# Sixteen strip copies of a fill, issued so that neighbours use different partition halves

## The reference, cut to what matters

```
x = x + L0_conv(group_norm(x))
t = to_tokens(x)                        # [16, 3136, 32]
t = t + attention(layer_norm(t))        # 32 features, softmax over 3136 keys
t = t + experts(layer_norm(t))          # top 2 of 8
x = from_tokens(t)

def L0_conv(x):                         # n c h w
    t1 = stack of x shifted by 2k-6 columns, k = 0..6
    t2 = conv(x, w2, 1x3)
    t3 = einsum('nakhw,nbhw->nakb', t1, x) / sqrt(h*w)
    t4 = stack of t2 shifted by k-3 rows, k = 0..6
    t7 = conv(t2, w7, 1x5, one filter per channel)
    t8 = conv(x, w8, 5x5, dilation 2, one filter per channel)
    t10 = einsum('nakb,nakhw->nbhw', p9w*p6w*t3, t4) / sqrt(c*7)
    return t8 - (t10 - t7)
```

## Time and profile before

| | |
|---|---|
| median of 3 runs | 2959.19 us |
| the profiled execution's own time | 2957.68 us |
| its span | 2955.7 us |
| busy: PE, DVE, ACT, POOL | 84%, 81%, 56%, 9% |
| first stage | 0 to about 655 us |
| copies of SyncE and ScalarE | 220.95 MB, mean 75 GB/s |

### The profile page before, as it was taken

The page is one execution under the profiler, slowest core; times in us unless marked ns, Lnnn a source line. Parts: engine busy times, 40 slices in busy tenths (PEclk is TensorE's granted clock), DMA queues, the critical chain, the costliest instruction groups (busy, mean ns, idle before and its releaser), DMA issues. The chain is left out here.

```text
span 2955.7 us, 47695 instructions
## 1 busy us (share of the span) xinstructions
PE 2474.4 (84%) x18582; PEld 990.8 (34%) x18582; DVE 2393.8 (81%) x4202; ACT 1649.4 (56%) x2170; POOL 276.4 (9%) x273
## 2 busy tenths in 40 slices
PE   3858585734599999999999999999999997787776
PEld 1332323210122222222222222222222226666664
DVE  4466666558899999999999999999999804888787
ACT  1243424350177777777777777777777793333322
POOL 0000000010000000000000000000000002454455
PEclk9989788855599999999999999999999995666667
DMA  7885859142001103110110110111010002221210
GB/s 167 186 218 163 221 157 240 72 157 74 1 1 56 56 1 116 56 37 20 56 56 1 56 56 15 42 56 56 1 56 23 4 20 77 69 96 66 99 66 22
DMA packets 61174, 220.95 MB, mean 75 GB/s; under 512 B 15526, under 2 KB 28450, under 8 KB 54306
## 3 DMA queue, kind: packets, MB, share of 16 engines
q1 hardware_dynamic: 59762, 214.41, 24.7%
q10 hardware_dynamic: 1200, 3.69, 0.3%
HBM read 81.67 MB, written 74.60 MB: 53 GB/s over the span
## 5 line engine op out<-in xcount | busy, mean ns | idle before, releaser
L1121 DVE TENSOR_REDUCE at_XM<-at_psX 128x1 f32<-128x448 f32 x2688 | 1551.9, 619 | 69.6 <-PE at_psX L1001 41.6
L1071 ACT ACTIVATE at_PR<-at_psS 128x896 f32<-128x896 f32 x1344 | 1159.3, 915 | 370.9 <-PE at_psS L980 368.6
L1017 PE MATMUL at_psV<-at_PR,at_V 128*32 128x448 f32 x5376 | 645.2, 552 | 0.5 <-ACT at_PR L1071 0.5
L980 PE MATMUL at_psS<-at_US,at_KS 128*128 128x448 f16 x2688 | 630.8, 356 | 2.5 <-ACT at_PR L1071 0.9
L1001 PE MATMUL at_psX<-at_KS,at_US 64*128 64x448 f16 x1344 | 501.9, 373 | 83.4 <-DVE at_XM L1121 76.7
L1001 PE MATMUL at_psX<-at_KS,at_UH 64*128 64x448 f16 x1344 | 501.8, 373 | 0.0
L1001 PEld LDWEIGHTS at_psX<-at_KS,at_US 64*128 64x128 f16 x1344 | 125.2, 93 | 751.9 <-DVE at_XM L1121 719.6
L980 PEld LDWEIGHTS at_psS<-at_US,at_KS 128*128 128x128 f16 x2688 | 205.1, 98 | 288.5 <-ACT at_PR L1071 140.4
L1396 POOL TENSOR_TENSOR fi_WE<-fi_WE 128x256 f32<-128x256 f32 (+1 forms) x224 | 212.8, 978 | 172.6 <-DVE fi_WE L1450 171.9
L393 PE MATMUL psA<-sb_stacks,sb_lhs 128*32 128x448 f32 x1568 | 170.2, 563 | 15.5 <-DVE sb_X L766 8.0
L1450 DVE TENSOR_TENSOR fi_WE<-fi_psE,fi_WT 128x512 f32<-128x512 f32 (+1 forms) x208 | 132.5, 665 | 43.4 <-PE fi_psE L1299 34.3
(11 more groups left out here) (186 smaller groups left out, 2000.5 us busy)
## 6 DMA issues: line engine op xcount, KB each, us to landing
sums<-at_O SPq DMA_DIRECT2D x16, 1568.0 KB, 6.3
fi_SUMS<-sums SPq DMA_DIRECT2D x16, 1568.0 KB, 6.6
sb_stacks<-sb_T SPq DMA_DIRECT2D x64, 270.5 KB, 5.8
sb_stacks<-sb_Xp SPq DMA_DIRECT2D x64, 248.8 KB, 5.0
sb_stacks<-sb_Xp SPq DMA_DIRECT2D x64, 248.0 KB, 4.9
at_KS<-key_stacks SPq DMA_DIRECT2D x16, 784.0 KB, 7.8
at_US<-query_stacks SPq DMA_DIRECT2D x16, 784.0 KB, 10.1
sb_stacks<-sb_T SPq DMA_DIRECT2D x64, 172.5 KB, 3.8
```

Of the source, the lines that this page charges most:

```text
L980: last = nc.tensor.matmul(psS[:, i % 2, j, 0:TILE], KS[:, b, c * P:(c + 1) * P], US[:, b, t * TILE:(t + 1) * TILE], start=True, stop=True)
L1017: last = nc.tensor.matmul(psV[C * q:C * q + C, 0:TILE], V[:, b, G * k + q, :], PR[:, (2 * q4 + q // 2) % PRS, q % 2, :], start=(k == 0), s ...
L1071: nc.scalar.activation(PR[:, (i - 2) % PRS], psS[:, i % 2, :, 0:TILE], ACT.Exp).then_inc(p_ready, 1)
L1121: nc.vector.tensor_reduce(o, psX[:, (at + j) % 3, 0:TILE], AX.X, ALU.max).then_inc(x_done, 1)
```

## The change

The two fills loop over one list of pairs instead of two nested loops. The same 16 copies are issued, with the same sizes, semaphores and waits before them; only their order within a fill differs.

```
+        HG = G // 2
+        STRIP_ORDER = [p for k in range(G) for j in range(HG) for p in ((j, (HG + j + k) % G), (HG + j, (j + k) % G))]
...
             def fill_stacks(g, h):
                 a, z = (0, XS_CUT) if h == 0 else (XS_CUT, XS_LEN)
-                for n in range(G):
-                    for s in range(G):
-                        sp.dma_start(XS[C * s:C * s + C, n, a:z],
-                                     Xp[C * n:C * n + C, 2 * s + a:2 * s + z]).then_inc(xs_in[h], 16)
+                for n, s in STRIP_ORDER:
+                    sp.dma_start(XS[C * s:C * s + C, n, a:z],
+                                 Xp[C * n:C * n + C, 2 * s + a:2 * s + z]).then_inc(xs_in[h], 16)
```

More of the change, by code:

```diff
@@ L274, in fill_stacks2 @@
                 sp.wait_ge(t2_ready, g * NT + (3 if h == 0 else NT))
[L275 to L278, removed]
+                for n, s in STRIP_ORDER:
+                    sp.dma_start(T2S[C * s:C * s + C, n, a:z],
+                                 T2[C * n:C * n + C, YW * s + a:YW * s + z]).then_inc(t2s_in[h], 16)
             def store(m, n, z=first, alone=False):
```

## The result

The changed kernel takes **2933.88 us** (median of 4 runs, 2933.05 to 2934.96), against 2958.86 us (2957.76 to 2959.78) for the kernel before in the same session: ratio 0.9918, 95% interval 0.9906 to 0.9931. That is 25 us less, where 49 were forecast, and 12 us above the top of the forecast's own range (2896 to 2922). The profiled execution took 2934.68 us with a span of 2932.7, 23.0 us less than before.

The account below looks back on a forecast made before the run. Bound by strip copies at 206 GB/s, on which TensorE and, through SyncE's queue, VectorE's token loads wait. Savings of 7.9 + 14.9 + 14.4 + 12.0 = 49.2 us over four passes gave 2910 us, range 2896 to 2922.

Parts of the forecast that it names:

- What bounds the kernel: Strip copies on SyncE's queue, at 206 GB/s, hold up TensorE's x strips and VectorE's token loads.
- That the sequencer is held back by the copies: SyncE's strip issue: median 1212 ns against shortest 582 ns, read as waiting for the copies ahead.
- The price of a strip: Time per x-stack strip: from 1.23 us to 0.80 us, taken between 0.70 and 0.92.
- The lone microsecond at 270 GB/s: First pass, 35 to 36 us, at the seam of strips 8 and 9: worth 0.31 us per seam.
- rival (a): Strip fills: a seam helps little, strips at 1.16 to 1.2 us, about 2949 us; chance 0.16.
- The passes: Savings forecast for the first four passes: 7.9, 14.9, 14.4 and 12.0 us, sum 49.2 us.
- The token wait of the third pass: VectorE's 11.7 us wait for the token load was to go, with 2.5 us to spare.
- the 1.6 us forecast there: Third pass, ScalarE's first eviction: held by a query store until 290.73, T2's clearing ends at 289.06.
- rival (b): Strip fills: half the gain, strips at 1.0 to 1.05 us, 30 us saved, 2929 us; chance 0.17.
- the five signs: 32 strips issued in about 26 us, rate near 300 GB/s, convolution at 38 to 39 us, short token waits, sb_T release.
- Over 1.1 us a strip: Strip fills: the forecast is wrong if a strip still takes over 1.1 us.
- The slower rival: Strip fills: the change costs time, each strip 4% (0.05 us) dearer, about +12 us, 2971 us; chance 0.05.

Follow-up runs that it names:

- short: Changed kernel with each strip cut to 8/11 of its columns (values not the reference's): 2905.84 us, 0.9833 of the kernel before.
- wide: Changed kernel with each x-stack fill as 4 copies over 128 partitions instead of 16 strips, without the quarter shift (values not the reference's): 2906.92 us, 0.9823.
- src_only: Changed kernel with another strip order: source half changes at every seam, destination half only after eight strips: 2957.34 us, 0.9998 of the kernel before.
- dst_only: Changed kernel with another strip order: destination half changes at all 15 seams, source half at one: 2958.43 us, 1.0001 of the kernel before.
- pairs: Changed kernel with both halves changing only after every second strip: 2945.67 us, 0.9961 of the kernel before.
- fours: Changed kernel with both halves changing only after the fourth and twelfth strips: 2961.0 us, 1.0016 of the kernel before.
- two_queues: Changed kernel with every second x strip of the first pass issued by ScalarE instead of SyncE: 2930.87 us, 0.9907 of the kernel before.
- tokens first: Changed kernel with image 0's residual, values and the next token load issued before the third fill: 2928.29 us, 0.9894 of the kernel before.
- quarters: Changed kernel with neighbouring strips in different quarters but four strips in each pair of halves: 2960.43 us, 1.0006 of the kernel before.

## Why the prediction was wrong, and where it was right

*What bounds the kernel* was right: *short* and *wide* take the token waits away by nothing but quicker strips, and end near 2906 us. *src_only* and *dst_only* confirm that both ends must change together, as the prediction argued from the steady 206 GB/s.

*That the sequencer is held back by the copies* was a wrong reading, though nothing in the sum came from it. In src_only the median issue is 593 ns while the copies run at 205 GB/s. The slow issue goes with neighbours that read from the same half, not with the rate; what holds it was not found.

*The price of a strip* is the step that failed: 0.80 us forecast, 1.13 measured (254 thousand bytes at 225 GB/s; 1.10 by the packets), outside even the 0.92 named as the cautious end. Two choices did it. The lone microsecond at 270 GB/s was taken for what each seam would give. It was the first change of the source half in the pass, which every order has once; rival (a) had called it a one-time filling, and that much of (a) came true. Nor was it the only full change in the trace before: the border of the two fills and the second fill have one each, and no two stand close together. *pairs* and *fours* measure about 0.1 us a seam. Then, from 0.92, I went further to 0.80, toward the 128-partition load, which has nothing in common with a row of strips.

*The passes.* With 0.12 us a strip for 0.43, the forecast's own arithmetic gives 16 x 0.12 = 1.9 us in the first pass (1.7 at the load of x) and 48 x 0.12 = 5.8 us in the third from fill to tokens (5.9). The token wait of the third pass was to vanish and is 7.3 us. The order of issues shows where. SyncE began the second x fill when the forecast had it (268.85; 279.3 less the 10.5 us of the earlier passes), but the third fill 25.5 us later and not 16.9. Of these 8.6 us, 16 x 0.33 = 5.3 are the price. The other 3.3 the forecast had put at nothing: the copy engines were still on strips of the first fill when the second was issued (to 273 us), and the third fill waits for the tokens copy. The token load then came 5.9 us after the fill, not 4.6, since SyncE waited 4.8 us, before 2.8, for the residual's copy, which was issued right behind the fill's strips. The remaining 1.6 us of that pass lie between VectorE's two token starts, 30.0 us before and 28.4 now: 0.7 at the second token load (1.14, now 0.45), the rest in waits for ScalarE. ScalarE's eviction is released by sb_T, as listed, but the third fill waited longer for the tokens copy, so the 1.6 us forecast there bought nothing by themselves.

Rival (a), strips at 1.16 us, had 3 us a pass and 2949; rival (b), 1.0 to 1.05 us, 2929. The kernel lies between them, nearer to (b) in time, though its strip (1.10 to 1.13) is dearer than (b) had it. Of the five signs, sb_T as releaser and the short issue appeared; the rate, the first convolution (43.17, not 38 to 39 us) and the token waits did not. "Over 1.1 us a strip" had been named as what would make it wrong: by the rate it was met, by the packets the strip stands at that bound.

*The slower rival* (c) fell: the stretches shown of the first pass are above the old rates. Its ground, 198 GB/s after the seam against 206 before, was an effect of where the stretch is cut; the packets' steps are 1.25 us on both sides.

The Trainium skill ("SBUF — State Buffer", section "Can I just issue two DMAs to hit both halves?") gives 6% for two concurrent copies in different halves. Here, with copies of one queue that change half at both ends, it is 9% and 13% in the two steady stretches, so the measurement decides against the figure; but the page's direction, that halves bring a few per cent and no doubling, was closer than my 1.23 to 0.80 us. The Trainium skill ("DMA: Bandwidth & Descriptors", section "Rules for kernel authors") also says that spreading copies over issuing engines does not help; two_queues agrees (229 against 225 GB/s).

## What to carry to other kernels

A short burst in a trace tells what one event gives in its own surroundings; before it is multiplied by sixteen, ask whether it is only the first of its kind, look for two such events in a row, or run one cheap order that has them. Price the resource by its rate in a steady stretch and not by how fast its issuer goes: here the issuer doubled its speed in src_only and the time did not move. And when a queue's order is changed to serve one waiter, list what else is held by the stores that move back; tokens first handed part of its wait to the keys (2928), keys with them did no better (2928), and only with ScalarE's copy moved too came 2922.5 us.

## What was not expected of the hardware

- An issue of a strip on SyncE takes 0.59 us by the median where neighbours read from different halves (src_only) and 1.21 us where they read from the same one (before 1.212, dst_only 1.216, quarters 1.180), at the same copy rate of 203 to 210 GB/s.
- Changing both halves at each seam gives 224 to 229 GB/s against 198 to 206; either half alone gives 203 to 210.
- The first change of the source half in a pass is followed by one step of 0.60 to 0.72 us, against 1.25, whatever the destination does. Later lone changes of both halves after eight strips from one source half gave 0.68 to 1.12 us in the first pass, close ones 1.10 to 1.16.
- Copies of the same bytes inside fast memory over 128 partitions: 421 GB/s.
- Copies issued far ahead hold up other engines' copies: the tokens copy of ScalarE landed 16.6 us after its issue in the third pass (7.8 before) and kept SyncE waiting 12.4 us, with the engines at a share of 1.02.
